# The output weights' gating and splitting, moved from VectorE to GpSimd and some blocks earlier

## The chip, the cores and the metric

The kernel runs on one core of a Trainium2 chip. The metric is the device time of one launch in microseconds (us); the profile is of one such execution, taken by the hardware profiler.

## The reference

Two transformer layers with AdaLN modulation run over 2048 tokens of width 512. The change lies in layer 0, between its causal attention (16 heads of 32) and its output projection:

```python
ctx = jnp.einsum('bhqk,bhkd->bhqd', probs, v)
ctx = ctx.transpose(0, 2, 1, 3).reshape(B, S, DIM)
return ctx @ W_out + b_out
...
x = x + ga * _L0_attn_ref(h, L0_attn_W_qkv, L0_attn_b_qkv, L0_attn_W_out, L0_attn_b_out)
h = _layernorm(x, axis=-1) * (1 + cb) + sb
x = x + gb * _L0_ffn_ref(h, L0_ffn_W1, L0_ffn_W2, L0_ffn_W3)
```

The gate `ga` is a row of 512 values. The kernel multiplies the columns of `W_out` and `b_out` by it, so that the projection's result can be added to `x` as it is.

## The kernel before

**Five queues.** Each engine has an instruction stream of its own, written out in program order; semaphores order the streams against each other. PE multiplies, ACT takes exponentials and casts, DVE (VectorE) takes maxima and splits, POOL (GpSimd) adds pairs of probability tiles, and SP issues the transfers.

**Attention.** It goes over 16 query blocks `n`, block n being head group n // 4 and 512 queries n % 4. Block n has 2 (n % 4 + 1) steps `(n, i)` of two key tiles each: blocks 12, 13, 14 and 15 have 2, 4, 6 and 8 steps. In a step PE makes eight score tiles (L1629), ACT the exponentials (L1718), PE the context (L1670). Instead of summing both key tiles' probabilities on PE, POOL adds them first (`add_pair`, L1586, four adds a step, one per head) and PE multiplies the sum by ones (L1649) two steps later. PE waits for `pair_ready` there.

**Maxima ahead.** The score maxima of a later block are made beside all this: PE issues a maxima matmul (L1190) between two score tiles, DVE reduces it (L1218). The matmuls rotate over three banks of PSUM, so a maxima matmul waits until the one three before it has been reduced. The maxima of block 15 are made in blocks 13 and 14 and end there; in block 15 DVE has only the finalization of block 14 (L1733 to L1744) and what stands behind it.

**Between attention and projection.** `prepare_vector` (L302 to L316) stands on DVE behind the finalization of block 14: four multiplications of `raw` (the weights, tile `o_raw`) by the gate row (L304), four casts to `w_hi` (L307), four subtractions to `w_lo` (L310), then for the first two halves of 256 tokens a cast `c_hi` (L313) and a subtraction `c_lo` (L328) of the context, and the gating of the bias (L267). The first multiplication waits for `early_loaded`, that is for the weights and for the gate row, which is loaded into `early_gate` once block 14 is finalized (L1542), since finalizations use that tile. Behind it DVE finalizes block 15. POOL, done with its pairs, adds the gated bias to the 16 residual tiles (`bias_gpsimd`, L299). PE's projection (L218 to L220) starts with half 0 when `w_ready` and `c_ready` allow. After halves 0 to 3 PE turns the first norm's `n_z` tiles (L174), which DVE makes (L163) after adding residuals (L349) and taking statistics (L137).

```python
if 2 <= slot < PRELUDE:
    pe.wait_ge(max_read, slot - 1)
elif slot >= PRELUDE + 3:
    pe.wait_ge(max_read, slot - 2)
```

Of the kernel before, what the change touches and what calls it, by code (L numbers as in the profile page):

```python
# [15 lines left out]
ALU = mybir.AluOpType  # L16
# [22 lines left out]
def build_program(nc, a, out):  # L39

    with ExitStack() as whole:
# [35 lines left out]
        OUT0, FFN0, QUERY1, OUT1, FFN1 = 32, 64, 80, 112, 144  # L77
# [148 lines left out]
        def project_out(ctx, alloc, tag, next_w, bias, src, src_ready, res_ready, there, raw=early_square):  # L226
# [21 lines left out]
            class Parts:  # L248
                ready = x_ready
                parts_ready = c_ready  # L250
                multiplied = proj

# [48 lines left out]
                def prepare_vector(dve, halves):  # L301
                    dve.wait_ge(early_loaded, there)  # L302
                    for k in range(KT):
                        nc.vector.tensor_tensor(raw[:, k, :], raw[:, k, :], gate, ALU.mult).then_inc(gated, 1)  # L304
                    for k in range(KT):
                        dve.wait_ge(gated, k + 1)
                        nc.vector.tensor_copy(w_hi[:, k, :], raw[:, k, :]).then_inc(w_hi_s, 1)  # L307
                    for k in range(KT):
                        dve.wait_ge(w_hi_s, k + 1)
                        nc.vector.tensor_tensor(w_lo[:, k, :], raw[:, k, :], w_hi[:, k, :], ALU.subtract).then_inc(w_ready, 1)  # L310
                    for i in range(halves):
                        src_ready(dve, i // 2)
                        nc.vector.tensor_copy(c_hi[:, i % 2, :, :], Parts.half(i)).then_inc(hi_s, 1)  # L313
                        Parts.lo_vector(dve, i)
                    Parts.bias_vector(dve)

# [669 lines left out]
        with ExitStack() as ctx:  # L986
# [506 lines left out]
            def attend_sync(sp):  # L1493
# [53 lines left out]
                sp.wait_ge(pairs_used, len(pair_index))  # L1547
                out_p.next_sync(sp)
                forward.sync(sp)

            def attend_gpsimd(pool):
# [45 lines left out]
                for s, (n, i) in enumerate(steps):  # L1597
                    if s in pair_index:
                        add_pair(s)
                    if not off_diagonal(s) and n in mixed_at:  # L1600
                        for step in range(0, 3) if i == 2 * (n % NB) else range(3, 8):
                            butterfly(8 * mixed_at[n] + step)
                pool.wait_ge(fw_stored, 16 * (D // FW))
# [117 lines left out]
            def attend_vector(dve):  # L1721
# [34 lines left out]
                out_p.prepare_vector(dve, 2)  # L1756
                for part in range(4):
# [6 lines left out]
                          "n2_rstd": 46 * KB + 224, "o0_w_hi": 48 * KB, "f0_d_hi": 48 * KB, "o0_w_lo": 56 * KB,  # L1764
# [251 lines left out]
```

## Time and profile before

| | us |
|---|---|
| median of 3 runs | 2014.23 |
| lowest, highest | 2013.72, 2018.39 |
| the profiled execution | 2016.38 |
| its span, first to last instruction | 2014.6 |

| engine | busy us | share |
|---|---|---|
| PE | 1929.0 | 96% |
| DVE | 1089.8 | 54% |
| ACT | 638.4 | 32% |
| POOL | 542.2 | 27% |

Times in a timeline are counted from the span's start. The start of an instruction is when its semaphores let it go; what it then waits for inside the engine counts in its duration. The mean granted clock of TensorE is 0.987 of full speed. Of the stages only a part concerns this change: blocks 12 to 15 of attention lie at 664 to 789 us, the output projection and its norm at 793 to 870 us.

### The profile page before, as it was taken

Reading aid. Unit: us, or ns where it says so; the run is one execution under the profiler, and the core shown is the slowest. Engines: PE = TensorE matmul, PEld = TensorE weight load, DVE = VectorE, ACT = ScalarE, POOL = GpSimd, SP = SyncE. Lnnn points to the kernel's source line nnn. Section 1 sums busy time; section 2 is a strip of 40 time slices with the busy share of each in tenths; the row PEclk is TensorE's granted clock in tenths of the full one; section 3 lists DMA queues with packets and bytes.
Section 4 is the critical chain, followed back from the end, with each engine's and each line's share of the span. In section 5 each row is a group of like instructions: output and inputs, shape, how many; then the busy total and the mean of one; then the engine's idle time right before and its main releaser. Section 6 shows DMA issues by size and latency. Waiting matters only on the chain. (4 is left out here: it accounts for less than half of the span.)

```text
span 2014.6 us, 25805 instructions
## 1 busy us (share of the span) xinstructions
PE 1929.0 (96%) x10068; PEld 1389.3 (69%) x10068; DVE 1089.8 (54%) x1834; ACT 638.4 (32%) x1157; POOL 542.2 (27%) x521
## 2 busy tenths in 40 slices
PE   6999999999999998899999999999999889999998
PEld 4677545545555544688888888887886678888886
DVE  4456776676666748863434443445432774434334
ACT  3231355555555564431111211113321241121111
POOL 0122578788686468300000000002000510000000
PEclk9999999999999999999999999999999999999999
DMA  9644422322321203110000000002000011000002
GB/s 316 215 158 146 101 54 55 73 66 55 85 43 34 54 12 105 58 43 32 5 28 32 32 21 12 0 19 71 8 6 11 21 53 32 32 21 21 6 1 84
DMA packets 61722, 111.87 MB, mean 56 GB/s; under 512 B 6000, under 2 KB 21248, under 8 KB 61568
## 3 DMA queue, kind: packets, MB, share of 16 engines
q1 hardware_dynamic: 54144, 85.05, 14.5%
q0 software_dynamic: 7456, 25.18, 4.2%
q8 instruction: 79, 1.29, 0.3%
q14 instruction: 43, 0.35, 0.1%
HBM read 84.77 MB, written 25.44 MB: 55 GB/s over the span
## 5 line engine op out<-in xcount | busy, mean ns | idle before, releaser
L1218 DVE TENSOR_REDUCE part_max<-banks 128x1 f32<-128x512 f32 (+2 forms) x640 | 356.8, 612 | 152.4 <-PE banks L1190 94.1
L1718 ACT ACTIVATE probs<-banks 128x512 f32<-128x512 f32 (+3 forms) x640 | 310.9, 539 | 275.1 <-PE banks L1629 134.2
L1190 PE MATMUL banks<-kst,qst 96*128 96x512 f32 (+2 forms) x640 | 262.4, 419 | 12.7 <-DVE part_max L1218 9.5
L1629 PE MATMUL banks<-qst,kst 98*128 98x512 f32 (+2 forms) x640 | 252.0, 414 | 0.2 <-ACT probs L1718 0.2
L711 DVE TENSOR_TENSOR tokens_a<-banks,tokens_a 128x512 f32<-128x512 f32 x224 | 151.2, 687 | 70.0 <-PE banks L220 69.2
L738 DVE TENSOR_TENSOR tokens_b<-banks,tokens_b 128x512 f32<-128x512 f32 x64 | 44.2, 691 | 251.7 <-ACT tokens_b L653 251.6
L1586 POOL TENSOR_TENSOR early_weights<-probs 128x512 f32<-128x512 f32 (+2 forms) x152 | 160.4, 1084 | 66.5 <-ACT probs L1718 66.1
L218 PE MATMUL banks<-f_d_hi,f_hid_hi 128*128 128x512 f32 x432 | 170.1, 394 | 7.6 <-DVE tokens_a L711 5.2
L1586 POOL TENSOR_TENSOR pairs_own<-probs 128x512 f32<-128x512 f32 (+2 forms) x152 | 158.1, 1069 | 71.1 <-ACT probs L1718 70.9
L218 PE MATMUL banks<-h_hi,f_w_first 128*128 128x512 f32 x448 | 174.6, 390 | 0.0
L220 PE MATMUL banks<-h_hi,f_w_first 128*128 128x512 f32 x448 | 174.3, 389 | 0.0
L219 PE MATMUL banks<-h_lo,f_w_first 128*128 128x512 f32 x448 | 174.3, 389 | 0.0
L1629 PEld LDWEIGHTS banks<-qst,kst 98*128 98x128 f32 x640 | 124.1, 195 | 64.3 <-issue 49.4
L219 PE MATMUL banks<-f_d_lo,f_hid_hi 128*128 128x512 f32 x432 | 168.2, 389 | 0.0
L220 PE MATMUL banks<-f_d_hi,f_hid_lo 128*128 128x512 f32 x432 | 168.2, 389 | 0.0
L1190 PEld LDWEIGHTS banks<-kst,qst 96*128 96x128 f32 x640 | 124.2, 195 | 59.9 <-DVE part_max L1218 45.8
L653 ACT ACTIVATE tokens_b<-banks 128x512 f32<-128x512 f32 x64 | 38.2, 597 | 395.7 <-PE banks L220 395.7
L218 PE MATMUL banks<-h_hi,f_w_second 128*128 128x512 f32 x416 | 161.9, 389 | 0.0
L219 PE MATMUL banks<-h_lo,f_w_second 128*128 128x512 f32 x416 | 161.9, 389 | 0.0
L220 PE MATMUL banks<-h_hi,f_w_second 128*128 128x512 f32 x416 | 161.8, 389 | 0.0
L858 POOL TENSOR_TENSOR w_lo<-early_weights,w_hi 128x512 fp32r<-128x512 f32 x4 | 5.1, 1303 | 544.7 <-ACT w_hi L832 544.7
L1670 PE MATMUL banks<-probs,tokens_a 128*32 128x512 f32 (+3 forms) x1280 | 141.9, 546 | 0.6 <-DVE tokens_b L1744 0.6
(199 smaller groups left out, 3271.2 us busy)
## 6 DMA issues: line engine op xcount, KB each, us to landing
tokens_a<-in_L_wmod SPq DMA_DIRECT2D x12, 1024.0 KB, 7.3
qst<-q_hi SPq DMA_DIRECT2D x32, 256.0 KB, 5.9
kst<-k_hi SPq DMA_DIRECT2D x32, 256.0 KB, 8.0
x<-in_L_attn_x SPq DMA_DIRECT2D x4, 1024.0 KB, 13.0
q_hi<-qk_out_hi POOLq DMA_DIRECT2D x16, 256.0 KB, 3.0
q_lo<-qk_out_lo POOLq DMA_DIRECT2D x16, 256.0 KB, 3.2
k_hi<-qk_out_hi POOLq DMA_DIRECT2D x16, 256.0 KB, 4.1
k_lo<-qk_out_lo POOLq DMA_DIRECT2D x16, 256.0 KB, 4.2
```

Source lines behind the costliest of these rows:

```text
L218: nc.tensor.matmul(dst, lh, rh, start=(first and i == 0), stop=False)
L219: nc.tensor.matmul(dst, lh, rl, start=False, stop=False)
L220: mm = nc.tensor.matmul(dst, ll, rh, start=False, stop=(last and i == n - 1))
L653: nc.scalar.activation(silu[:, u % 2, :], bank[2 * (u % 2)][:], ACT.Silu, scale=1.0 if mixed else gs[:, ch:ch + 1]).then_inc(silu_s, 1)
L711: nc.vector.tensor_tensor(xt, bank[4 + n % 3][:], xt, ALU.add).then_inc(x_added, 1)
L738: nc.vector.tensor_tensor(act_[:, u % 2, :], up_bank, silu[:, u % 2, :], ALU.mult).then_inc(hid_s, 1)
L1190: mm = nc.tensor.matmul(dst[:, 0:wide], qst[n % QS][0:BIASROW, h, P * t:P * t + P], kst[(NB * g + c) % KS][0:BIASROW, h, 0:wide], start=Tr ...
L1218: nc.vector.tensor_reduce(part_max[:, n % 2, ht, c:c + 1], max_bank(slot)[:, 0:wide], AX_X, ALU.max).then_inc(max_read, 1)
L1586: nc.gpsimd.tensor_tensor(pairs[o % 2][:, h, c0:512], probs[:, 2 * s % PS, h, c0:512], probs[:, (2 * s + 1) % PS, h, c0:512], ALU.add).the ...
L1629: mm = nc.tensor.matmul(dst[:, c0:512], kst[ck % KS][0:BIASROW + 2, h, at:at + P], qst[n % QS][0:BIASROW + 2, h, c0:512], start=True, stop ...
L1670: mm = nc.tensor.matmul(bank[6][HD * h:HD * h + HD, c0:512], v[:, kt, at:at + HD], probs[:, q % PS, h, c0:512], start=(kt == 0), stop=(las ...
L1718: nc.scalar.activation(probs[:, q % PS, h, c0:512], score_bank(sh)[:, c0:512], ACT.Exp, scale=SCALE).then_inc(exp_done, 1)
```

## The change

The gate row gets a tile of its own (`gate_row`, tile `o_gate`), loaded together with the weights, both right behind the keys and queries of block 15 in SP's queue and ahead of the rows of block 14's maxima. POOL multiplies the four weight tiles by it behind the pairs of steps (12, 1) and (13, 2), and makes `w_lo` behind those of (13, 3), (14, 0) and (14, 1), and `c_lo` of half 0 behind those of (14, 2). DVE keeps the casts, now among the maxima: `w_hi` at the ends of steps (13, 1), (13, 2) and (14, 0), `c_hi` at the ends of (14, 1) and (14, 3). Behind the finalization of block 14 DVE keeps two instructions, the bias and `c_lo` of half 1.

```diff
-                def prepare_vector(dve, halves):
+                def gate_gpsimd(pool, k, row):
+                    if k == 0:
+                        pool.wait_ge(early_loaded, there - 16)
+                    nc.gpsimd.tensor_tensor(raw[:, k, :], raw[:, k, :], row, ALU.mult).then_inc(gated, 1)
+
+                def weight_hi_vector(dve, k):
+                    dve.wait_ge(gated, k + 1)
+                    nc.vector.tensor_copy(w_hi[:, k, :], raw[:, k, :]).then_inc(w_hi_s, 1)
+
+                def weight_lo_gpsimd(pool, k):
+                    pool.wait_ge(w_hi_s, k + 1)
+                    if k == 0:
+                        pool.wait_ge(gated, KT)
+                    nc.gpsimd.tensor_tensor(w_lo[:, k, :], raw[:, k, :], w_hi[:, k, :], ALU.subtract).then_inc(w_ready, 1)
+
+                def context_hi_vector(dve, i):
+                    src_ready(dve, i // 2)
+                    nc.vector.tensor_copy(c_hi[:, i % 2, :, :], Parts.half(i)).then_inc(hi_s, 1)
+
+                def context_lo_gpsimd(pool, i):
+                    pool.wait_ge(hi_s, i + 1)
+                    nc.gpsimd.tensor_tensor(c_lo[:, i % 2, :, :], Parts.half(i), c_hi[:, i % 2, :, :],
+                                            ALU.subtract).then_inc(c_ready, 1)
+
+                def rest_vector(dve):
                     dve.wait_ge(early_loaded, there)
...
                     Parts.bias_vector(dve)
+                    dve.wait_ge(c_ready, 1)
+                    Parts.lo_vector(dve, 1)
...
-                    if n == NQ - 1 and not is_load:
-                        sp.wait_ge(score_mm, 4 * quads_before(NQ - NB))
+                    (load if is_load else rows_of_max)(n)
+                    if n == NQ - 1 and is_load:
                         sp.dma_start(raw0, tile_rows(a["w_out0"])).then_inc(early_loaded, 16)
-                    (load if is_load else rows_of_max)(n)
+                        sp.dma_start(gate_row, gates[0:1, :].broadcast_to([P, D])).then_inc(early_loaded, 16)
...
+                sp.wait_ge(out_p.bias_multiplied, 1)
                 out_p.next_sync(sp)
...
+            GATED = {(12, 1): (0, 1), (13, 2): (2, 3)}
+            WEIGHT_HI = {(13, 1): (0,), (13, 2): (1,), (14, 0): (2, 3)}
...
```

On DVE, blocks 13 and 14 before, from the last piece of the finalization of block 12 on (the rows named `part_max` are reductions of maxima, `tokens_b` is the context):

```order
L1744 TENSOR_TENSOR tokens_b<-banks,early_gate 128x512 [waits fw_stored,fin_step]
L1218 TENSOR_REDUCE part_max<-banks 128x1 [waits max_mm] x34
L1733 STREAM_TRANSPOSE early_gate<-banks 128x512 [waits pairs_used,probs_read]
L1218 TENSOR_REDUCE part_max<-banks 128x1 [waits max_mm]
L1736 RECIPROCAL turned_rec<-early_gate 128x16 [waits fin_step]
L1218 TENSOR_REDUCE part_max<-banks 128x1 [waits max_mm]
L1739 STREAM_TRANSPOSE early_gate<-turned_rec 128x512 [waits fin_step]
L1218 TENSOR_REDUCE part_max<-banks 128x1 [waits max_mm]
L1744 TENSOR_TENSOR tokens_b<-banks,early_gate 128x512 [waits fin_step]
L1218 TENSOR_REDUCE part_max<-banks 128x1 [waits max_mm] x20
```

Now, the same stretch in block 13:

```order
L1772 TENSOR_TENSOR tokens_b<-banks,early_gate 128x512 [waits fw_stored,fin_step]
L1233 TENSOR_REDUCE part_max<-banks 128x1 [waits max_mm] x12
L309 CAST o_w_hi<-o_raw 128x512 [waits o0_w_gated_s]
L1233 TENSOR_REDUCE part_max<-banks 128x1 [waits max_mm] x10
L309 CAST o_w_hi<-o_raw 128x512 [waits o0_w_gated_s]
L1233 TENSOR_REDUCE part_max<-banks 128x1 [waits max_mm] x12
```

and in block 14, from the last piece of the finalization of block 13 to the end of the maxima:

```order
L1772 TENSOR_TENSOR tokens_b<-banks,early_gate 128x512 [waits fin_step]
L1233 TENSOR_REDUCE part_max<-banks 128x1 [waits max_mm]
L309 CAST o_w_hi<-o_raw 128x512 [waits o0_w_gated_s] x2
L1233 TENSOR_REDUCE part_max<-banks 128x1 [waits max_mm] x8
L319 CAST o_c_hi<-tokens_b 128x1024 [waits ctx_done]
L1233 TENSOR_REDUCE part_max<-banks 128x1 [waits max_mm] x11
L1242 TENSOR_REDUCE neg_max<-part_max 128x16 [waits max_mm,max_read]
```

Five casts now stand among the reductions, and behind each of them come reductions that PE waits for; the second `c_hi` stands behind the rows of block 15's maxima.

On DVE, between the finalizations of blocks 14 and 15, now; before, 17 instructions stood in the place of the two in the middle, the bias last:

```order
L1772 TENSOR_TENSOR tokens_b<-banks,early_gate 128x512 [waits fin_step]
L268 TENSOR_TENSOR o_bias<-o_bias,early_gate 128x512 [waits o0_bias_loaded,early_loaded]
L343 TENSOR_TENSOR o_c_lo<-tokens_b,o_c_hi 128x1024 [waits o0_c_hi_s,o0_c_ready]
L1761 STREAM_TRANSPOSE pairs_own<-banks 128x512 [waits pairs_used,probs_read]
L1764 RECIPROCAL turned_rec<-pairs_own 128x16 [waits fin_step]
```

What is left are the bias and `c_lo` of half 1, and both have two inputs in SBUF.

On POOL, from the last adds of step (13, 2) to `w_lo` 2; before, only the rows of L1608 stood there (L1586 then):

```order
L1608 TENSOR_TENSOR early_weights<-probs 128x384 [waits exp_done] x3
L305 TENSOR_TENSOR o_raw<-o_raw,o_gate 128x512 x2
L1608 TENSOR_TENSOR pairs_own<-probs 128x128 [waits exp_done,pairs_used]
L1608 TENSOR_TENSOR pairs_own<-probs 128x128 [waits exp_done] x3
L315 TENSOR_TENSOR o_w_lo<-o_raw,o_w_hi 128x512 [waits o0_w_gated_s,o0_w_hi_s]
L315 TENSOR_TENSOR o_w_lo<-o_raw,o_w_hi 128x512 [waits o0_w_hi_s]
L1608 TENSOR_TENSOR early_weights<-probs 128x512 [waits exp_done,pairs_used]
L1608 TENSOR_TENSOR early_weights<-probs 128x512 [waits exp_done] x3
L315 TENSOR_TENSOR o_w_lo<-o_raw,o_w_hi 128x512 [waits o0_w_hi_s]
```

Of the nine instructions that are new on POOL five stand here, each behind a step's four adds and ahead of the next step's.

## Rows read from the trace of the kernel before

**Rows 1.** Who PE waited for from 789 to 900: us in total, times, longest.

```profile
PE banks L218 <- DVE o_c_lo L328: 4.1, 1, 4.1
```

**Rows 2.** PE's timeline, 785 to 820: start us, us, instruction, [idle before <-releaser].

```profile
788.60 0.43 PE L1649 MATMUL banks<-pairs_own,ones 128*32 128x128 f32 x8 [1.41 <-POOL pairs_own L1586]
...
793.15 0.80 PE L218 MATMUL banks<-o_w_hi,o_c_hi 128*128 128x512 f32 x1 [4.13 <-DVE o_c_lo L328]
...
818.94 1.09 PE L174 MATMUL banks<-ident,n_z 128*128 128x128 f32 x8 [2.38 <-DVE n_z L163]
```

**Rows 3.** By stretch: us, busy of PE, PEld, DVE, ACT, POOL, then PEclk, DMA, GB/s.

```profile
793.00:796.00 3.00, 2.85 (x7) 2.27 (x8) 2.96 (x5) 0.00 (x0) 0.30 (x1) 0.50 0.90 300
...
800.00:810.00 10.00, 10.00 (x46) 8.29 (x45) 5.51 (x5) 3.38 (x3) 10.00 (x7) 1.00 0.00 1
```

**Rows 4.** DVE's timeline, 754 to 833.

```profile
754.92 31.53 DVE L304 TENSOR_TENSOR o_raw<-o_raw,early_gate 128x512 f32<-128x512 f32 x4 [3.47 <-DMA early_gate<-gates]
...
786.37 2.46 DVE L307 CAST o_w_hi<-o_raw 128x512 fp32r<-128x512 f32 x4
...
794.88 0.68 DVE L267 TENSOR_TENSOR o_bias<-o_bias,early_gate 128x512 f32<-128x512 f32 x1
...
806.85 2.26 DVE L328 TENSOR_TENSOR o_c_lo<-tokens_b,o_c_hi 128x1024 fp32r<-128x1024 f32 x1 [3.75 <-ACT o_c_hi L324]
...
814.56 4.32 DVE L163 TENSOR_SCALAR n_z<-tokens_a,n_mv,n_rstd 128x512 f32<-128x512 f32 x4
...
831.76 1.92 DVE L163 TENSOR_SCALAR n_z<-tokens_a,n_mv,n_rstd 128x512 f32<-128x512 f32 x4
```

**Rows 5.** Tile o_raw: min/median/max ns, first and last start.

```profile
L304 DVE TENSOR_TENSOR o_raw<-o_raw,early_gate x4: 677/678/29723, 754.9 to 785.8; 128x512 f32<-128x512 f32 x4
```

**Rows 6.** POOL's timeline, 746 to 818.

```profile
746.40 1.70 POOL L1586 TENSOR_TENSOR pairs_own<-probs 128x128 f32<-128x128 f32 x4 [1.81 <-ACT probs L1718]
...
750.04 5.12 POOL L1586 TENSOR_TENSOR early_weights<-probs 128x512 f32<-128x512 f32 x4 [1.94 <-ACT probs L1718]
...
780.15 3.94 POOL L1586 TENSOR_TENSOR early_weights<-probs 128x384 f32<-128x384 f32 x4
...
785.90 2.65 POOL L1586 TENSOR_TENSOR pairs_own<-probs 128x128 f32<-128x128 f32 x4 [1.80 <-ACT probs L1718]
...
795.70 22.45 POOL L299 TENSOR_TENSOR tokens_a<-tokens_a,o_bias 128x512 f32<-128x512 f32 x16 [7.15 <-issue]
```

**Rows 7.** POOL's timeline in blocks 13 and 14.

```profile
690.44 5.00 POOL L1586 TENSOR_TENSOR pairs_own<-probs 128x512 f32<-128x512 f32 x4 [3.36 <-ACT probs L1718]
...
698.29 3.97 POOL L1586 TENSOR_TENSOR early_weights<-probs 128x384 f32<-128x384 f32 x4 [2.85 <-ACT probs L1718]
...
711.94 5.09 POOL L1586 TENSOR_TENSOR early_weights<-probs 128x512 f32<-128x512 f32 x4 [3.77 <-ACT probs L1718]
...
719.33 5.00 POOL L1586 TENSOR_TENSOR pairs_own<-probs 128x512 f32<-128x512 f32 x4 [2.30 <-ACT probs L1718]
```

**Rows 8.** DVE's reductions of maxima in blocks 13 and 14.

```profile
689.94 5.54 DVE L1218 TENSOR_REDUCE part_max<-banks 128x1 f32<-128x512 f32 x10 [1.45 <-PE banks L1190]
...
697.95 5.34 DVE L1218 TENSOR_REDUCE part_max<-banks 128x1 f32<-128x512 f32 x9 [2.47 <-PE banks L1190]
...
714.44 3.06 DVE L1218 TENSOR_REDUCE part_max<-banks 128x1 f32<-128x512 f32 x5
...
718.82 4.34 DVE L1218 TENSOR_REDUCE part_max<-banks 128x1 f32<-128x512 f32 x8 [1.32 <-PE banks L1190]
```

**Rows 9.** PE's timeline in step (13, 2).

```profile
693.69 0.70 PE L1190 MATMUL banks<-kst,qst 96*128 96x512 f32 x2
```

**Rows 10.** Line L203, a cast of DVE with POOL at rest.

```profile
L203 DVE CAST ht_hi<-n_h x8: 418/420/420, 24.0 to 151.0; 128x512 fp32r<-128x512 f32 x8
```

**Rows 11.** The transfer of the weights: KB, us to landing.

```profile
o_raw<-in_w_out SPq DMA_DIRECT2D x1, 1024.0 KB, 5.2
```

More of the change, by code:

```diff
@@ L76, in build_program @@
         early_gate = sb(whole, "early_gate", [P, D])
-        OUT0, FFN0, QUERY1, OUT1, FFN1 = 32, 64, 80, 112, 144
+        OUT0, FFN0, QUERY1, OUT1, FFN1 = 48, 80, 96, 128, 160
         x = tokens_a
@@ L251, in project_out @@
                 multiplied = proj
+                bias_multiplied = bias_gated
                 def sync(sp):
@@ L299, in bias_gpsimd @@
                         nc.gpsimd.tensor_tensor(x[:, t, :], x[:, t, :], bias_row[:], ALU.add).then_inc(xb_ready, 1)
-                def prepare_vector(dve, halves):
-                    dve.wait_ge(early_loaded, there)
[L303 to L314, printed above, removed]
+                def gate_gpsimd(pool, k, row):
+                    if k == 0:
+                        pool.wait_ge(early_loaded, there - 16)
+                    nc.gpsimd.tensor_tensor(raw[:, k, :], raw[:, k, :], row, ALU.mult).then_inc(gated, 1)
@@ L1547, in attend_sync @@
                 sp.wait_ge(pairs_used, len(pair_index))
+                sp.wait_ge(out_p.bias_multiplied, 1)
                 out_p.next_sync(sp)
                 forward.sync(sp)
+            GATED = {(12, 1): (0, 1), (13, 2): (2, 3)}
+            WEIGHT_HI = {(13, 1): (0,), (13, 2): (1,), (14, 0): (2, 3)}
+            WEIGHT_LO = {(13, 3): (0, 1), (14, 0): (2,), (14, 1): (3,)}
+            CONTEXT_HI = {(14, 1): (0,), (14, 3): (1,)}
+            CONTEXT_LO = {(14, 2): (0,)}
             def attend_gpsimd(pool):
@@ L1602, in attend_gpsimd @@
                             butterfly(8 * mixed_at[n] + step)
+                    for k in GATED.get((n, i), ()):
+                        out_p.gate_gpsimd(pool, k, gate_row)
+                    for k in WEIGHT_LO.get((n, i), ()):
+                        out_p.weight_lo_gpsimd(pool, k)
+                    for half in CONTEXT_LO.get((n, i), ()):
+                        out_p.context_lo_gpsimd(pool, half)
                 pool.wait_ge(fw_stored, 16 * (D // FW))
@@ L1755, in attend_vector @@
                             max_vector(dve, slot)
-                out_p.prepare_vector(dve, 2)
+                    for k in WEIGHT_HI.get((n, i), ()):
+                        out_p.weight_hi_vector(dve, k)
+                    for half in CONTEXT_HI.get((n, i), ()):
+                        out_p.context_hi_vector(dve, half)
+                out_p.rest_vector(dve)
                 for part in range(4):
@@ L1769, in build_program @@
             res_loaded = [sem(ctx, f"res_loaded{b}") for b in range(NB)]
+            gate_row = alloc("o0_gate", [P, D])[:]
             raw0 = alloc("o0_raw", [P, KT * D])[:].rearrange("p (k d) -> p k d", k=KT)
```

2 lines of the change are left out of this document (1 added, 1 removed).

## The prediction

> **What bounds the kernel now.** PE is busy 96% of the span, so a change pays only where PE waits. I read the list of waits first: behind attention PE waits once, 4.1 us, for `c_lo` on DVE [rows 1]. The timeline of PE gives the place [rows 2]: the sums of block 15 are issued at 788.60, after 1.41 us of waiting for POOL, PE is done at 789.03, and the projection starts at 793.15. The stretches show what follows: from 793 to 796 TensorE's granted clock is 0.50, the lower level of 1.2 GHz, and 7 matmuls fall into 3 us; from 800 to 810, at 1.00, 46 fall into 10, counting the two cut by its ends [rows 3]. PE had stood still for 4 us before the clock fell. The next wait on the way is 2.38 us for `n_z` [rows 2].
>
> Why is `c_lo` late? DVE's timeline has a row of 31.53 us for four multiplications of `o_raw` [rows 4], and the tile's own line says that one took 29.7 us and the others 0.68 [rows 5]. It is let go at 754.92 and ends at 784.64. Over that time POOL adds pairs without a gap, from 750.04 to 784.09 [rows 6]. So a DVE instruction with two SBUF inputs did not get through beside POOL until POOL paused. From then DVE needs 10.9 us to the end of the bias (to 795.5), and POOL, which waits for the bias, starts its 16 residual adds at 795.70.
>
> **What the change takes away.** Of the 17 instructions behind block 14's finalization two remain. They will still hang until 784.05, like the one before, and then need 0.60 + 1.15 us: done at about 785.8, ahead of PE's last sums.
>
> 1. The wait of 4.13 us goes: `w_lo` and half 0's `c_lo` are finished in block 14.
> 2. POOL's last group is four adds of 128 columns. It took 2.65 us beside DVE's casts; the same group in block 14, with DVE idle, took 1.70 [rows 6]. DVE is now out of the way, so PE's wait of 1.41 shrinks by 0.95. 0.46 us of it stays, and then PE has work.
> 3. PE no longer stands still before the projection. 7 matmuls were busy for 2.85 us of the 3, so one took 0.41 to 0.43 us instead of 10 / 45 = 0.22 (the two cut ones counted as one): 1.3 to 1.5 us; bounds 0 (the clock falls anyway somewhere near) and 1.4. I take 1.4.
> 4. The bias adds start at 787.6 instead of 795.70, 8.1 us earlier, while PE starts 5.1 us earlier, so they get out of the norm's way by 3 us. `n_z` took 4.32 us beside POOL's adds and 1.92 in the next block without them [rows 4]. They end at 787.6 + 22.45 = 810.1 (22.45 from [rows 6]). PE arrives at `n_z` after 96 matmuls at 0.227 us (10 / 44, the cut ones left out), 788.1 + 21.8 = 809.9. `n_z` started 814.56 - 793.15 = 21.4 us behind the projection, of which 1.4 was the slow clock, so now at 788.1 + 20.0 = 808.1; two of its microseconds still lie beside POOL, and I take 2.7 us for it: 810.8, a wait of 0.9 instead of 2.38, worth 1.5; bounds 0 and 2.4.
>
> Together 4.13 + 0.95 + 1.4 + 1.5 = 8.0 us; bounds 5.1 (the first two) and 8.9. The rest of the projection and the first feed-forward hang on PE and shift with it. The new wait of SP for the bias holds back the next stage's weights, but they were issued at 791.3 only, behind `w_lo`, and come earlier now.
>
> **What it adds in blocks 12 to 14.** On POOL: eight operations of 1.25 us (an add of this shape is 5.00 / 4) and one of 2.5. POOL's idle times before the next groups are 2.30 to 3.77 us [rows 7], and in block 14 at most 2.5 us is put into one of them, so its own queue hides them; without that cover each microsecond too much would delay the pairs that PE sums two steps later, where it has several to spare. The transfer of the weights (5.2 us [rows 11]) now runs behind block 15's keys and ahead of (12, 1)'s end; the first product may wait for it on POOL a microsecond or two, which the same slack takes. I cost both at nothing.
>
> On DVE the casts stand among maxima for which PE waits, since a maxima matmul needs the reduction three before it. There is no slack: in step (13, 2) PE issues its last two together at 693.69 [rows 9] while DVE's row of ten, 0.6 us each, runs from 689.94 to 695.48 [rows 8]. So the time by which DVE comes late in such a phase is PE's, once for each phase. A cast alone takes 0.42 us [rows 10], `c_hi` of twice the width about 0.6. What it waits for POOL is the unknown. Between ends:
> - No waiting: 0.4 + 0.35 + 0.7 (two casts) + 0.55 = 2.0 us.
> - A wait to the end of the running POOL instruction. The cast of (13, 1) comes after five of the ten reductions, at 692.94; POOL's adds end at 691.7, 692.97 and 694.2 [rows 7], so 0 to 1.25 us of waiting, in the middle 0.6, in all 1.05. The cast of (13, 2) comes after five of the nine, at 700.8, and the add ends at 701.28: 0.8 with the cast. Those of (14, 0) come after one reduction, at 715.04; the third add ends at 715.75, the first cast runs, the fourth add runs, the second cast ends at 717.85: 2.65. `c_hi` comes after four of the eight, at 720.96, and the add ends at 721.86: 1.45. Sum 5.95, of which 0.6 either way is open.
> - A wait until POOL pauses, as in the 29.7 us: until 695.44, 704.8 (two products follow the adds), 717.03 and 725.6 (a `w_lo` follows): 2.9 + 4.3 + 2.7 + 5.2 = 15.1 us.
>
> I take the middle. Two rows speak for it. While POOL's group of four was stretched from 1.70 to 2.65 us, DVE's four casts had a pitch of 0.60 instead of 0.42 [rows 4, 6]: they took turns, instruction by instruction. And `c_lo` at 806.85 took 2.26 us, about 1.2 of work plus the rest of one residual add [rows 4]. Against it stands the one multiplication that (784.05 - 754.92) / 1.25 = 23 boundaries between POOL's adds did not let through, and it stood beside the very adds of 512 columns that the new casts meet. The Trainium skill (SBUF — State Buffer, "Who interferes with whom") says that GpSimd and a DVE cast in a 2-port mode, or a DVE operation with two SBUF inputs, take one port pair for a whole instruction, and that the later one blocks until the first finishes. By that rule the cost is the middle case, 5.95 us; by the 29.7 us of [rows 5], which it does not explain, it is 15.1.
>
> **The sum.** 5.95 - 8.0 = -2.0 us. The profiled execution took 2016.38 (span 2014.6) and would take 2014.4; it lies 2.15 above the median of the runs, 2014.23, which becomes 2012.2.
>
> **The rivals.**
> - *DVE starves (slower).* The casts wait until POOL pauses, 15.1 - 8.0 = +7.1 us: 2021.3. For it: [rows 5]. Against: the turns of [rows 4, 6]. The place is PE's maxima matmuls in steps (13, 2), (13, 3) and (14, 2), and it decides from a cost of 14 us on, that is if at least the casts of (13, 2) and (14, 1) wait for a pause.
> - *The casts cost their own time only.* They find gaps, or need not wait: 2.0 - 8.0 = -6.0: 2008.2. For it: a cast's arrival moves when PE has been held up, and POOL pauses for 2.30 to 3.77 us ahead of each group [rows 7]. Against: a step's last maxima and POOL's adds of that step begin together.
> - *DVE's next work takes the place of the wait.* The projection starts early, but its chain of `c_lo`, residual adds, statistics and `n_z` is as long as before and the low clock comes elsewhere: 5.1 of the 8.0 remain, 5.95 - 5.1 = +0.9: 2015.1.
> - *The change doesn't do what it says*: a late gate row or a crowded POOL queue delays `w_lo` beyond block 14. PE would then wait in block 15 or as before, near 2014 plus the casts' cost, 2020 at most. The gaps of [rows 7] speak against it.
>
> **How the numbers follow.** Middle case 0.43, starving 0.25, own time only 0.20, DVE next 0.09, not as said 0.03. A measurement of this kernel tells 0.3% (6.04 us) from no change, so faster means below 2008.2 and slower above 2020.3. Faster: half of the own-time case, which lies on the bound, and the tail of the middle case with 8.9 us of gain and few waits, 0.10 + 0.08 = 0.18. Slower: three fifths of starving and a little of the last, 0.17. Within: 0.65. The range goes from 8.9 - 2.0 = 6.9 us below (2007.3) to 15.1 - 8.0 = 7.1 above (2021.3), which leaves out about one in ten at either end.
>
> **What the changed profile would show.** PE's row of 4.13 us before L218 is gone and no stretch at 0.50 begins there (steps 1, 3); the wait before PE's last sums is about 0.5 (2); POOL's residual adds start within a microsecond of its last pairs and PE's wait for `n_z` is near 1 (4). The casts' durations decide the rest: 0.42 us each for the own-time case, 0.5 to 1.7 for the middle one, 2 to 5 for starving, with PE waiting for `part_max` by as much. I would be wrong if PE's waits for maxima in blocks 13 and 14 did not grow, if the bias got through between POOL's adds in block 15 and held them up, or if POOL's adds began late in block 14.

## The result, and the profile after

The changed kernel took 2032.07 us in the median of five executions (2024.77 to 2035.22), against 2014.23 for before in the same comparison (2011.71 to 2018.39, five executions). The ratio is 1.0064, with a 95% interval from 1.0037 to 1.009: slower, by 0.64% (the two medians alone are 0.89% apart). The prediction was 2012.2 us, with a range from 2007.3 to 2021.3; the time lies above it, and the sign is the other one. The profiled execution took 2032.2 us, its span is 2030.4. Ratios, here and below, are over the executions in the faster of the two states; one execution of before, of 6566.74 us in the comparison of e5 to e8, is in the other.

I read the waits of PE first, from 600 to 900 us (us in total, times, longest). Before, in the same stretch:

```profile
PE banks L218 <- DVE o_c_lo L328: 4.1, 1, 4.1
...
PE banks L174 <- DVE n_z L163: 2.6, 2, 2.4
...
PE banks L1190 <- DVE part_max L1218: 2.1, 6, 0.5
```

and after:

```profile
PE banks L1205 <- DVE part_max L1233: 9.8, 10, 3.9
PE banks L218 <- DVE o_c_lo L343: 9.4, 1, 9.4
PE banks L218 <- DVE tokens_a L364: 4.2, 2, 3.6
```

The wait of [rows 1] is gone, and two others stand in its place: 7.7 us more for the maxima, and 9.4 us for a `c_lo` again, not that of half 0 but a later one. PE's timeline says where (start us, us, instruction, idle before and releaser), as in [rows 2]:

```profile
701.36 0.79 PE L1205 MATMUL banks<-kst,qst 96*128 96x512 f32 x1 [3.87 <-DVE part_max L1233]
...
720.25 0.80 PE L1205 MATMUL banks<-kst,qst 96*128 96x512 f32 x1 [2.26 <-DVE part_max L1233]
...
795.86 0.43 PE L1677 MATMUL banks<-pairs_own,ones 128*32 128x128 f32 x8 [0.46 <-POOL pairs_own L1608]
796.21 0.50 PE L218 MATMUL banks<-o_w_hi,o_c_hi 128*128 128x512 f32 x1
...
816.77 0.80 PE L218 MATMUL banks<-o_w_hi,o_c_hi 128*128 128x512 f32 x1 [9.38 <-DVE o_c_lo L343]
```

The projection follows PE's last sums without a stop, where before PE stood 4.13 us. But PE has waited 3.87 us for maxima behind the rounding of step (13, 2), and 2.26 behind those of (14, 0); it is half a step ahead of DVE there, in (13, 3) and (14, 1). And it stops again in the middle of the projection. DVE's timeline has the causes, as [rows 4] had:

```profile
687.19 1.55 DVE L309 CAST o_w_hi<-o_raw 128x512 fp32r<-128x512 f32 x1
...
696.54 4.17 DVE L309 CAST o_w_hi<-o_raw 128x512 fp32r<-128x512 f32 x1
...
717.00 2.59 DVE L309 CAST o_w_hi<-o_raw 128x512 fp32r<-128x512 f32 x2
...
728.18 1.02 DVE L319 CAST o_c_hi<-tokens_b 128x1024 fp32r<-128x1024 f32 x1
...
763.90 28.95 DVE L268 TENSOR_TENSOR o_bias<-o_bias,early_gate 128x512 f32<-128x512 f32 x1 [4.29 <-DMA early_gate<-gates]
...
803.14 14.71 DVE L343 TENSOR_TENSOR o_c_lo<-tokens_b,o_c_hi 128x1024 fp32r<-128x1024 f32 x2 [0.47 <-ACT o_c_hi L339]
```

The last row is two instructions; the tile's own line gives 13572 ns for the longest and 1211 for the shortest. Beside them stands POOL, as in [rows 6, 7]:

```profile
694.02 3.97 POOL L1608 TENSOR_TENSOR early_weights<-probs 128x384 f32<-128x384 f32 x4 [4.14 <-ACT probs L1746]
697.92 2.50 POOL L305 TENSOR_TENSOR o_raw<-o_raw,o_gate 128x512 f32<-128x512 f32 x2
...
713.90 5.07 POOL L1608 TENSOR_TENSOR early_weights<-probs 128x512 f32<-128x512 f32 x4 [1.28 <-ACT probs L1746]
719.34 1.38 POOL L315 TENSOR_TENSOR o_w_lo<-o_raw,o_w_hi 128x512 fp32r<-128x512 f32 x1 [0.37 <-DVE o_w_hi L309]
...
795.76 19.88 POOL L300 TENSOR_TENSOR tokens_a<-tokens_a,o_bias 128x512 f32<-128x512 f32 x16
```

The rounding of 696.54 ended at 700.7, when POOL's two products ended at 700.4; the `c_lo` of 803.14 ended at 816.7, when POOL's sixteenth residual add ended at 815.6. Both got through when POOL stopped, not at the ends of its instructions; below I call that starved. The roundings of 717.00 did so, too: the first of the two took 2.26 us, from inside POOL's third add (it ended at 717.71) to 719.25, behind the end of the fourth (718.97), and the second 0.41. Those of 687.19 and 728.18 went through at the next end of an add. The stretches (columns as in [rows 3], the one before the last two is PEclk) show what PE's stops did to TensorE:

```profile
696.00:700.00 4.00, 1.50 (x10) 0.91 (x8) 4.00 (x3) 1.31 (x4) 4.00 (x5) 0.88 0.00 0
...
702.00:705.00 3.00, 3.00 (x17) 0.80 (x20) 1.10 (x2) 0.00 (x0) 0.00 (x0) 0.50 0.00 0
...
696.00:730.00 34.00, 26.42 (x157) 13.42 (x155) 24.68 (x36) 13.01 (x28) 19.03 (x19) 0.80 0.00 0
...
818.00:820.00 2.00, 2.00 (x6) 1.52 (x6) 1.97 (x4) 0.00 (x0) 0.00 (x0) 0.50 0.00 0
```

PE stood idle, and then ran at 0.50, the level of 1.2 GHz. Before, the stretch from 696 to 730 had 1.00 all through.

**Where the time went, place by place.** The two profiled executions were already 5.7 us apart (after ahead) when block 13 began, by low clocks long before any change, so absolute times mislead. I take four marks that both traces have and compare the distances between them: POOL's group of step (13, 1), POOL's first group in block 15, DVE's first add of the projection, and the 21st of DVE's adds into `tokens_a` or `tokens_b` behind attention. Before they stand at 690.44, 750.04, 797.87 and 875.91, after at 684.70, 758.21, 799.27 and 889.58.

| stretch against before, us | changed kernel |
|---|---|
| blocks 13 and 14 | +13.9 |
| block 15 and the turn to the projection | -6.8 |
| projection and first feed-forward | +12.3 |
| together | +19.4 |

These distances have one execution of before to stand against, and they leave out what lies outside the marks.

So the gain was there, and two losses lie around it.

### The profile page after: what moved, and what is told of

Its sections match the earlier page's. It is cut to its first block and busy times, and to the rows that moved or that the text cites. A ratio compares the mean times of both kernels' runs of the same rounds, so it can differ in the third digit from the quotient of the medians.

```text
span 2030.4 us, 25809 instructions
## 1 busy us (share of the span) xinstructions
PE 1936.0 (95%) x10068; PEld 1391.5 (69%) x10068; DVE 1099.9 (54%) x1825; ACT 638.5 (31%) x1157; POOL 552.3 (27%) x530
## 5 line engine op out<-in xcount | busy, mean ns | idle before, releaser
L1608 POOL TENSOR_TENSOR pairs_own<-probs 128x512 f32<-128x512 f32 (+2 forms) x152 | 157.8, 1068 | 72.5 <-ACT probs L1746 72.2
L1608 POOL TENSOR_TENSOR early_weights<-probs 128x512 f32<-128x512 f32 (+2 forms) x152 | 160.4, 1084 | 60.7 <-ACT probs L1746 60.3
```

Source lines behind the costliest of these rows:

```text
L1608: nc.gpsimd.tensor_tensor(pairs[o % 2][:, h, c0:512], probs[:, 2 * s % PS, h, c0:512], probs[:, (2 * s + 1) % PS, h, c0:512], ALU.add).the ...
```

## The experiments

Each kernel below is the changed one with the edit shown, unless it says otherwise. Ratios are to the kernel before, executed on the same chip, with 95% intervals. The table at the end has the marks of all of them.

**The roundings on ACT (e1).** `copy` of ACT in the place of `tensor_copy` of DVE, at the same steps:

```diff
-                    nc.vector.tensor_copy(w_hi[:, k, :], raw[:, k, :]).then_inc(w_hi_s, 1)
+                    nc.scalar.copy(w_hi[:, k, :], raw[:, k, :]).then_inc(w_hi_s, 1)
...
-                    nc.vector.tensor_copy(c_hi[:, i % 2, :, :], Parts.half(i)).then_inc(hi_s, 1)
+                    nc.scalar.copy(c_hi[:, i % 2, :, :], Parts.half(i)).then_inc(hi_s, 1)
```

> The changed kernel with its six roundings (w_hi 0 to 3, c_hi 0 and 1) issued on ACT at the same steps instead of on DVE; all else as changed. Theory A: in blocks 13 and 14 the changed kernel lost 14.0 us against before (the same ACT result was 5.9 us earlier before block 13's second step and 8.2 us later behind block 14), because DVE's roundings wait for POOL (4.17 us for the one of step (13, 2)), PE stands 3.87 and 2.26 us for the maxima, and then runs at a granted clock of 0.50. ACT's copies do not wait for POOL, so PE's waits for maxima fall to about 2 us over the blocks and the low clock goes: about 2032 - 13 = 2019 (2016 to 2022), above before by the wait of c_lo in the projection, which stays. Rival B, the loss comes from POOL's longer queue or the earlier weight transfers and not from DVE's roundings: 2030 to 2033, PE still waits. Rival C, ACT's copies (about 0.6 us each) delay the exponentials: 2022 to 2026 with PE waiting for probs.

Measured: 2009.33 us, ratio 0.9987 (0.9968 to 1.0006). Blocks 13 and 14 cost 3.2 us more than before instead of 13.9. ACT's copies took 0.61 us each beside the same adds of POOL; the Trainium skill (SBUF — State Buffer, "SBUF: two separate sides") says that ACT never waits for another engine's port, and this trace agrees. Rival B falls: the products and the transfers are still there. About half of the 3.2 us are waits of PE for `probs`, behind copies that stand between exponentials: 1.6 us instead of the 0.2 of before and of the changed kernel. That is rival C, in small. The rest is a stretch at the lower clock (0.57 from 728 to 732), where before had 1.00. The time lies 10 us under what I expected, and that was the first sign that the `c_lo` is not always starved. Here it was not:

```profile
PE banks L1657 <- ACT probs L1746: 1.6, 3, 0.8
...
788.94 1.25 DVE L343 TENSOR_TENSOR o_c_lo<-tokens_b,o_c_hi 128x1024 fp32r<-128x1024 f32 x1 [0.47 <-ACT o_c_hi L339]
```

**`c_lo` of halves 2 and 3 on POOL (e2).** The two subtractions come ahead of residual adds 6 and 10 in POOL's own order, and DVE leaves them out:

```diff
                     for t in range(T):
+                        if t in split_before:
+                            pool.wait_ge(c_ready, split_before[t])
+                            Parts.context_lo_gpsimd(pool, split_before[t])
                         res_ready(pool, t)
...
-                    out_p.bias_gpsimd(pool)
+                    out_p.bias_gpsimd(pool, {6: 2, 10: 3})
```

> The changed kernel with c_lo of halves 2 and 3 subtracted by POOL between its residual adds (ahead of the adds of rows 6 and 10) instead of by DVE. Theory A: in the changed kernel DVE's c_lo of half 2 was let go at 803.15 and got through only when POOL was done at 815.6 (13.57 us), PE stood 9.38 us and then ran at 0.50 for another 6 us of work; as POOL's own instruction c_lo takes 2.4 us in the queue, from about 803.3 to 805.7, and PE needs it at 807.1. So the wait and the low clock go: about 2032 - 11 = 2021 (2018 to 2024). Rival D, DVE's later work (its adds from the banks, the norm) is delayed by POOL all the same and the wait moves to the first n_z: 2026 to 2030. Rival E, the 13.57 us was chance of this one profiled execution and the median never held it: no change, 2029 to 2033.

Measured: 2018.66 us, ratio 1.0013 (0.9997 to 1.003). The projection and feed-forward cost 0.3 us more than before instead of 12.3, so rival D falls. Rival E does not fall by this run: the changed kernel has 1.4 when its `c_lo` happens not to be starved (e5, below), and its median of 2019.63 (e9) is near this one. Blocks 13 and 14 repeat to a tenth (+13.9), with the same 4.17 us for the same rounding.

**Both edits (e3).**

> Both edits together: the roundings on ACT and c_lo of halves 2 and 3 on POOL. If the two losses of theory A are separate and add up: 2032 - 13 - 11 = 2008 (2004 to 2012), below before (2014) by the 6 to 8 us that the prediction counted as gains. If one hides behind the other, or the gain before the projection is given back in the norm: 2012 to 2018.

Measured: 2009.65 us, ratio 0.9971 (0.9958 to 0.9983). Blocks +3.1, turn -6.7, projection +1.5: the two losses are separate.

**The roundings alone, in the kernel before (e4).** No work is moved; six spare roundings are added at the changed kernel's places:

```diff
+                    for k in WEIGHT_HI.get((n, i), ()):
+                        out_p.spare_weight_cast(dve, k)
+                    for half in CONTEXT_HI.get((n, i), ()):
+                        out_p.spare_context_cast(dve, half)
                 out_p.prepare_vector(dve, 2)
```

> The kernel before with nothing but six spare roundings added on DVE at the places of the changed kernel: w_hi of the still ungated weights (4) and c_hi (2), overwritten by the real ones in block 15 as before. Theory A: the roundings alone bring the loss, since the adds of POOL that they meet are those of before: PE waits 3 to 4 us more for a maximum at step (13, 2) and 2 us at (14, 0), with stretches at 0.50 behind them: 2014 + 10 to 14 = 2024 to 2028. The middle case of the prediction (a rounding waits for the one running POOL instruction): 2014 + 6 = 2020. Rival B (POOL's added work or the transfers are to blame): 2014 to 2016.

Measured: 2021.84 us, ratio 1.0037 (1.0024 to 1.0051). The roundings alone make before slower, by 7.6 us in blocks 13 and 14. PE waited 6.9 us for maxima instead of 2.1, and the granted clock was 0.97 over the two blocks. The time is near the prediction's middle case. Of DVE's rows that of (13, 2), which took 4.17 us in the changed kernel, is that case: it went through at the next end of an add. The first rounding of (14, 0) is not: 2.25 us, to the pause behind the group's last add, as in all seven executions with a rounding on DVE at that place (2.23 to 2.26).

```profile
685.71 1.56 DVE L304 CAST o_w_hi<-o_raw 128x512 fp32r<-128x512 f32 x1
...
695.07 0.74 DVE L304 CAST o_w_hi<-o_raw 128x512 fp32r<-128x512 f32 x1
```

**The changed kernel again (e5, one profiled execution; e9, timed).**

> The changed kernel itself, profiled once more. Theory A (the waits for POOL are set by the program's own timing): the roundings of DVE take again about 1.56, 4.17, 2.26 us and PE waits 3.9 and 2.3 us at steps (13, 2) and (14, 0); the c_lo of half 2 is either starved again (13.6 us, PE waits 9.4) or let through in 1.2 to 2.3 us, and then this execution is 11 to 12 us shorter. In the kernel with the roundings on ACT the same c_lo, 1.17 us into a residual add of POOL, got through in 1.25 us, in the changed kernel, 1.11 us into one, it did not; so I give no more than even odds.

> The changed kernel once more, timed in five rounds, since its profiled executions fell into two kinds: 2032.2 (c_lo of half 2 starved for 13.57 us) and 2018.4 (the same c_lo through in 1.23 us). Theory A: its executions lie in two groups some 12 us apart, near 2018 to 2022 and near 2030 to 2034, and the median says only which group has more of them; the five of the result had four at 2031 to 2035 and one at 2024.8. With both groups mixed: median 2019 to 2032. Rival G: the c_lo has nothing to do with the spread, the executions of one chip lie within 8 us of each other wherever they lie.

Measured: e5 took 2018.39 us; e9 2019.63 in the median, ratio 1.0016 (1.000 to 1.0032). The roundings of blocks 13 and 14 came out alike each time (4.16 and 4.18 us for that of (13, 2)), but the `c_lo` did not. In e5 it was let go 1.17 us into a residual add and took 1.23 us. In the profiled execution of e9 it was let go 1.13 us into one and was starved (two instructions in this row):

```profile
803.89 14.70 DVE L343 TENSOR_TENSOR o_c_lo<-tokens_b,o_c_hi 128x1024 fp32r<-128x1024 f32 x2 [0.47 <-ACT o_c_hi L339]
```

That execution took 2031.5 us; nine others of e9 lie between 2018.2 and 2022.6, two at 2010.2 and 2012.4. So the executions fall in groups, and rival G is wrong. Four of the result's five lie in the upper group; of e1's twelve, three lie at 2020.5 to 2021.1, one at 2015.1, the others between 2007.4 and 2011.1. Only two of these executions were seen in a profile; that the others of the upper groups were starved too is inferred from the time. With that inference it is 8 of 30 over the result, e1, e5 and e9. The inference is weak for times up to 2022: e2, whose `c_lo` is POOL's own, spreads from 2009.86 to 2022.86, and before from 2010.94 to 2022.78 beside it. Why the first comparison had four of five and e9 one of twelve stays open.

**POOL pauses where DVE needs its turn (e6).**

```diff
+                    if (n, i) == (13, 2):
+                        pool.wait_ge(out_p.rounded, 2)
                     for k in GATED.get((n, i), ()):
...
                     for t in range(T):
+                        if t in pause_before:
+                            pool.wait_ge(c_ready, pause_before[t] + 1)
                         res_ready(pool, t)
```

> The changed kernel with POOL made to pause where DVE needs its turn: at step (13, 2) POOL waits for DVE's second rounding before its two products, and its residual adds of rows 6 and 10 wait for c_lo of halves 2 and 3. No work is moved. Theory A (DVE's instruction gets in when POOL stops issuing): the rounding of (13, 2) ends with POOL's fourth add, 1.4 us instead of 4.17, PE's wait there 1.1 instead of 3.87 and no low clock behind it, worth 2.8 + 2.7 = 5.5 us; c_lo of half 2 takes 1.2 to 1.4 us at 803.3, PE does not wait, worth 9.4 + 2.6 = 12 where it was starved: 2032 - 17 = 2015 (2012 to 2018). Rival F, DVE is starved for another reason than POOL's unbroken issue: the 4.17 and 13.6 us stay, POOL waits with them, 2032 or more.

Measured: 2018.29 us, ratio 1.0005 (0.9986 to 1.0023). The rounding of (13, 2) took 1.73 us where it had taken 4.17, and POOL's products followed it:

```profile
696.22 1.73 DVE L312 CAST o_w_hi<-o_raw 128x512 fp32r<-128x512 f32 x1
```

The blocks cost 9.3 us more than before instead of 13.9. So at (13, 2) it is POOL's unbroken issue that keeps DVE out, and a pause lets it in; the end of POOL's third add was passed by here, too. Of the expected 5.5 us 4.6 came; the 12 us for `c_lo` were a comparison with a starved execution. The `c_lo` of half 2, let go 1.17 us into an add, took 1.23 us, as it did in e5 without a pause.

**ACT's roundings in the middle of the steps (e7).** On top of both edits, behind the exponentials of a step's first half:

```diff
+                        if half == 0:
+                            for k in WEIGHT_HI.get((n, i), ()):
+                                out_p.weight_hi_scalar(act, k)
...
-            WEIGHT_HI = {(13, 1): (0,), (13, 2): (1,), (14, 0): (2, 3)}
+            WEIGHT_HI = {(13, 1): (0,), (13, 2): (1,), (13, 3): (2,), (14, 0): (3,)}
...
-            CONTEXT_HI = {(14, 1): (0,), (14, 3): (1,)}
+            CONTEXT_HI = {(14, 1): (0,), (14, 2): (1,)}
```

> The kernel with both edits (2009.65), its roundings on ACT moved from the end of a step to the middle, behind the exponentials of the step's first half, where ACT stands idle 2 to 4 us, one for each step from (13, 1) to (14, 2). In the kernel with both edits PE waited 1.6 us for probs behind the roundings at steps (14, 0), (14, 1) and (14, 3) and lost 3.2 us against before in these blocks (the ACT result went from 7.5 us ahead to 4.3 ahead). If those waits come from the roundings' places: they go, 2009.65 - 3.2 = 2006.5 (2004 to 2009). If ACT is short of time wherever they stand: 2009 to 2011.

Measured: 2009.32 us, ratio 0.996 (0.9947 to 0.9973). Blocks 13 and 14 cost nothing any more (0.0), with all of POOL's added work still in them. The median hardly moved against e3, but the chip of this comparison was slower (before: 2018.24).

**DVE's roundings in the middle of the steps (e10).** The same places on DVE, behind the maxima of a step's first half, with `c_lo` on POOL:

> The changed kernel with c_lo of halves 2 and 3 on POOL (so that it cannot be starved) and DVE's roundings kept on DVE, but moved from the end of a step to its middle, behind the maxima of the step's first half, where both DVE and POOL stand idle for 1 to 3 us; the same places that the roundings on ACT had when blocks 13 and 14 cost nothing. Theory A (what costs is meeting POOL's adds, with maxima queued behind): the roundings take 0.42 us each, PE's waits for maxima stay at 1.6 us, the blocks cost 0 to 1 us more than before instead of 13.9: 2018.7 - 13 = 2006, or in this call's terms 5 to 9 us under before. Rival H (the roundings cost PE wherever they stand among the maxima, by DVE's own queue): at least 3 us of the 13.9 stay. Rival: they meet the end of POOL's group in one or two of the steps: 2009 to 2012.

Measured: 2009.48 us, ratio 0.9965 (0.9952 to 0.9978), blocks 0.0. Same engine, same instructions as the change, a few microseconds earlier (the first 2.0 us ahead of POOL's group of step (13, 1), where it was 2.5 us behind the group's start):

```profile
681.43 0.41 DVE L312 CAST o_w_hi<-o_raw 128x512 fp32r<-128x512 f32 x1
...
688.40 0.42 DVE L312 CAST o_w_hi<-o_raw 128x512 fp32r<-128x512 f32 x1
...
696.55 1.49 DVE L312 CAST o_w_hi<-o_raw 128x512 fp32r<-128x512 f32 x1 [0.24 <-POOL o_raw L308]
...
703.42 0.55 DVE L312 CAST o_w_hi<-o_raw 128x512 fp32r<-128x512 f32 x1
```

Even the 1.49 us cost PE nothing: DVE had to wait for PE behind it, 1.12 us, for the next maxima. Its waits for maxima are those of before:

```profile
PE banks L1212 <- DVE part_max L1240: 2.0, 6, 0.5
```

Rival H falls.

**Spare instructions beside block 15 (e8).** Nine spare instructions on DVE, on top of both edits:

```diff
+                    for probe in range(9):
+                        dve.wait_ge(probed, probe)
+                        if probe < 3:
+                            mm = nc.vector.tensor_copy(c_hi[:, 1, 0:2, :], some)
+                        elif probe < 6:
+                            mm = nc.vector.tensor_scalar(c_lo[:, 1, 0:2, :], some, 1.0, None, ALU.mult)
+                        else:
+                            mm = nc.vector.tensor_tensor(c_lo[:, 1, 0:2, :], some, some, ALU.subtract)
+                        mm.then_inc(probed, 1)
```

> The kernel with both edits and nine spare instructions on DVE behind block 14's finalization, beside POOL's gapless adds of block 15, each on 128x512 in SBUF and each waiting for the one before: three roundings (one input), three multiplications by 1.0 (one input and a constant, float32), three subtractions with two inputs in SBUF; then the bias multiplication as before. If only instructions with two SBUF inputs are starved beside adds of 512 columns (the multiplications of o_raw and of the bias were, 6 times of 6), the first six take 0.4 to 1.7 us each and the seventh about 20 us. If any DVE instruction that shares the port can be, the first rounding may take the whole 28 us. If each takes its turn, all take 0.4 to 2 us. The time tells little: 2008 to 2012, more where PE has to wait behind.

Measured: 2021.76 us in its one execution. The first rounding, with one input, took the whole time:

```profile
754.89 29.38 DVE L337 CAST o_c_hi<-tokens_b 128x512 fp32r<-128x512 f32 x3 [4.47 <-DMA early_gate<-gates]
...
800.20 2.47 DVE L137 BATCH_NORM_STATS2 n_stats<-tokens_a 128x6 f32<-128x512 f32 x4
...
802.99 11.90 DVE L147 TENSOR_SCALAR n_ve<-n_mv 128x4 f32<-128x4 f32 x1
```

Of the 29.38 us one of the three has 28.45, the others 0.43 each. So one input is enough; it does not take the two of the multiplications in [rows 4, 5]. The multiplications by 1.0 and the subtractions came behind it, when POOL's gapless row was over, and show nothing. The last row came unasked: an instruction of 128x4 elements, 0.17 us by itself, was kept out for 11.90 us beside POOL's residual adds and its `c_lo`. So a small one can be kept out, too. But not every kind is: the four statistics just ahead of it, 128x512 each, took 2.47 us together beside the same adds, 0.62 from start to start.

**Spare roundings with a semaphore (e11).** e4 with a wait, already met, and an increment on each rounding:

```diff
+                    dve.wait_ge(early_loaded, there - 16)
+                    nc.vector.tensor_copy(w_hi[:, k, :], raw[:, k, :]).then_inc(spare, 1)
```

> The kernel before with the six spare roundings, each now with a semaphore wait (already met) and an increment, as the real ones have. Open: in the kernel with spare roundings the one of step (13, 2) got through at the next boundary between POOL's adds (0.75 us), in the changed kernel in four profiles of four it did not (4.16 to 4.18), though it stood 0.55 us into an add of 1.02 us in each. If the wait or the increment decides: it takes 1.7 us here, to the pause behind POOL's fourth add, and PE waits 1 us more. If what decides is what POOL has queued behind (two products there, nothing here) or the moment to a few hundredths of a microsecond: 0.75 us again or 1.7 by chance; then one profile can't tell these two apart, and it stays open.

Measured: 2038.54 us in its one execution. The rounding of (13, 2) took 1.74 us, to the pause behind POOL's fourth add. The moment within the add does not tell the two forms apart: the spare rounding of e4 was let go 0.555 us into it and got through at its end, that of the changed kernel 0.554 us into it and did not, nor did this one at 0.543. With one profile for either form of the spare rounding, whether the semaphore decides stays open. What it shows beyond doubt is the `c_lo` in a kernel with the order of before, let go 0.41 us into a residual add (two instructions again):

```profile
808.73 15.42 DVE L337 TENSOR_TENSOR o_c_lo<-tokens_b,o_c_hi 128x1024 fp32r<-128x1024 f32 x2 [0.47 <-ACT o_c_hi L333]
```

The first of the two has 14.28 us. So this starving does not need the moved work; the order of before, with spare roundings some 100 us earlier, has it too. In before's own profile the same `c_lo` went through.

**Roundings in the middle of the steps, pauses for `c_lo` (e12).** e10's places and e6's pauses ahead of residual adds 6 and 10; nothing goes to another engine.

> The changed kernel with DVE's roundings in the middle of the steps and, in place of c_lo on POOL, POOL's pauses for DVE's c_lo of halves 2 and 3: nothing is moved to another engine. Theory A: as with c_lo on POOL, 5 to 9 us under before, no execution 12 us above the others; perhaps 1 us more, since DVE's c_lo comes ahead of its adds and norm. If c_lo is starved in spite of the pause: some executions at 2020 to 2022.

Measured: 2007.34 us (2004.86 to 2013.28, nine executions), ratio 0.9963 (0.9951 to 0.9975). This beats both kernels: 0.37% under before. Among the 37 timed executions of e3, e7, e10 and e12, whose `c_lo` is guarded in one way or the other and whose roundings cost little, the highest is 2014.65. That is no proof for the guard: e2 and e6 are guarded as well, and reach 2022.86 and 2026.92.

**The marks of all kernels**, each from its profiled execution, in us against before. Where `c_lo` was not starved and there are medians, these lie 1.6 to 4.3 us lower against before's than the last column says (e2: +3.7 instead of +7.4), so the columns are better compared with each other than with the ratios.

| kernel | blocks 13, 14 | turn | projection | together |
|---|---|---|---|---|
| changed | +13.9 | -6.8 | +12.3 | +19.4 |
| e9, changed again | +13.3 | -6.8 | +11.9 | +18.4 |
| e5, changed again | +13.3 | -6.7 | +1.4 | +7.9 |
| e2, `c_lo` on POOL | +13.9 | -6.8 | +0.3 | +7.4 |
| e6, pauses | +9.3 | -6.7 | +1.8 | +4.4 |
| e4, spare roundings | +7.6 | +0.8 | +0.7 | +9.1 |
| e11, with semaphores | +10.2 | +0.6 | +13.0 | +23.7 |
| e1, ACT | +3.2 | -6.7 | +1.3 | -2.2 |
| e3, both | +3.1 | -6.7 | +1.5 | -2.1 |
| e7, ACT between | 0.0 | -6.8 | +0.4 | -6.4 |
| e10, DVE between | 0.0 | -6.8 | +1.5 | -5.3 |
| e12, between and pauses | 0.0 | -6.8 | +0.4 | -6.4 |
| e8, spare instructions | +1.6 | -4.3 | +5.0 | +2.3 |

## Why the prediction was wrong

**Steps 1 to 3, the gain at the turn: right.** They gave 4.13 + 0.95 + 1.4 = 6.5 us, and every kernel with the moved preparation shows 6.7 or 6.8, but for e8, whose spare instructions stand there (4.3). PE's wait for POOL's last group is 0.46, the value taken.

**Step 4, the norm: right in the wait, wrong in the worth.** In the execution without starving (e5) PE waits 0.92 us for `n_z`, where I said 0.9, and the stretch at 0.50 behind it is gone. But the 1.5 us did not arrive: the projection and feed-forward cost 1.4 us more than before. The low clock came elsewhere. PE's old wait of 3.62 us for `tokens_a` is in both kernels. Before, PEclk stayed at 1.00 behind it; in e5 it did not. First before:

```profile
844.00:848.00 4.00, 2.34 (x10) 1.99 (x11) 3.97 (x7) 0.00 (x0) 2.88 (x3) 1.00 0.25 71
```

and e5, where that wait ends at 842.99:

```profile
844.00:848.00 4.00, 4.00 (x11) 3.13 (x10) 3.66 (x13) 0.21 (x1) 0.21 (x1) 0.50 0.82 253
```

So of what a removed stop gives back, the part for the clock is uncertain: the trace of before did not say which of two stops the clock would follow. The bound of 0 in step 4 was too high by 1.4 us. In e5 6.7 - 1.4 = 5.3 of the 8.0 us are left, near the 5.1 of the rival that had the low clock come elsewhere, to which I gave 0.09.

**The roundings in blocks 13 and 14: the step that failed.** I took 5.95 us; it was 13.9. Two things are in the difference. First, the price of a meeting. The middle case, a wait for the running instruction of POOL, fits two of the four places: 1.55 us at (13, 1) where I had 1.05, and 1.02 at (14, 1) where I had 1.45. At (13, 2) it was 4.17 instead of 0.8, which is the starving rival's 4.3. At (14, 0) the two roundings took 2.59 where I had 2.65, but by the other path: the first hung past an end of an add until POOL paused (2.26 us) and the second was free (0.41), while I had let them in one by one. The rival had 2.7 there, so the total could not tell the two apart, and that it came out is luck. By the Trainium skill's rule (SBUF — State Buffer, "SBUF: two separate sides") the later instruction waits until the first finishes; the rows of (13, 1) and (14, 1) agree, and the 4.17, the 2.26 and the 28.45 us do not, since one or more of POOL's instructions finished meanwhile. Together DVE came 9.3 us late, and PE waited 7.7 us more. Second, the clock. I counted it where a stop of PE was taken away (step 3), and nowhere where one was added. The remaining 13.9 - 7.7 = 6.2 us are for the most part PE at 0.50: a mean of 0.80 over the 34 us from 696 to 730 is 13.6 us at the lower level, which costs half of that where PE has work, 6.8 us at most (PE stood for a part of it). The same two terms account for the other profiles within about 1 us, e5 by 8.0 more of waiting and a mean clock of 0.93 over 72.9 us, at most 5.1 us, against 13.3. This term was missing in all of my cases, in the starving rival's 15.1 too, which therefore came near the truth for the wrong reason.

Two slips of the prediction's own sums change nothing of this: the second rounding's end at 717.85 would make (14, 0) 2.81 and not 2.65, and waits for a pause at (13, 2) and (14, 1) alone would have made 5.95 + 3.5 + 3.75 = 13.2 us, short of the 14 from which it said it was slower.

**What no case had: the starved `c_lo`.** I read its 2.26 us [rows 4] as the rule beside residual adds, and moved on. PE stood 9.38 us for it, and the stretch at 0.50 behind it cost more: 12.3 us for the stage, against 1.4 in e5. I had the instrument for it: the same two engines, the same kind of adds without a gap, and a row of 29.7 us. I gave starving a chance of 0.25, but only for the roundings. The rival priced some places of a mechanism that can work wherever DVE meets a gapless row of POOL.

**The signs.** Without starving the changed kernel is slower by 7.9 us of marks (e5), or by the ratio of 1.0016 (1.000 to 1.0032) in e9; with it by 18 to 19. To slower by over 0.3% the prediction gave 0.17; the result's comparison is above that, e9's is not. The missing clock term alone would have moved its likeliest case from -2.0 to about +4 (an estimate, with the 6.2 us from above).

**What stays open.** Whether a DVE instruction gets through at the first end of a POOL instruction or not until a pause. In block 15 all fourteen profiled executions, before among them, kept DVE's first such instruction out (28.45 to 30.17 us each). Beside the residual adds DVE's `c_lo` mostly went through, and was starved in the changed kernel, e9 and e11, let go 1.11, 1.13 and 0.41 us into an add; others got through from 0.11, 0.60, 0.71 and 1.17 us into one. The rounding of (13, 2) was let go between 0.53 and 0.56 us into the third add in seven executions, and got through at its end in one (e4). I found no rule in these numbers. Nor is it shown why the clock follows one stop of 3.6 us and not another.

## What to carry to other kernels

Before putting DVE work beside POOL, look at what is queued behind it and whether POOL pauses: a rounding of 0.4 us cost nothing in a gap of both engines, and took up to 4.2 us a few microseconds later, nearly all of it PE's time, with a stretch at the lower clock behind it. Where DVE must get through a long row of POOL instructions, put a wait for its result into POOL's queue or give the instruction to POOL or ACT. And price the clock for every stop of PE that a change adds, not only for those that it removes.

## What the runs showed of the hardware that I had not expected

- DVE was kept out by POOL's unbroken issue with instructions of several kinds: a rounding with one input (28.45 us, e8), a multiplication with two (28.95), a `tensor_scalar` of 128x4 elements (11.90, e8). Statistics of 128x512 were not (0.62 each, e8). Its wait is then set by POOL's next pause, and a pause made by a semaphore was enough at (13, 2) (1.73 us instead of 4.17, e6).
- It is bistable from one execution of a kernel to the next: the same `c_lo` took 1.23 us in e5 and 13.57 in the changed kernel, 10.9 us by the marks of the stage.
- The granted clock of 0.50 that is saved behind one stop of PE may turn up behind another that had none before (1.00 and 0.50 from 844 to 848).
